# Fewer stored copies of the split delta and delta*u rows, and twice as many, shorter loads of the scan's matrices

## What is computed

```python
def step(h, inputs):
    d_t, B_t, C_t, u_t = inputs
    dA = jnp.exp(d_t[:, :, None] * A)
    h = h * dA + (d_t * u_t)[:, :, None] * B_t[:, None, :]
    y_t = jnp.einsum('bdn,bn->bd', h, C_t)
    return (h, y_t)
```

## Time and profile before

| | |
|---|---|
| median of 3 runs | 6699.06 us |
| the profiled execution's own time | 6696.66 us |
| its span in the trace | 6694.9 us |
| busy share over the span | PE 89%, DVE 82%, ACT 50%, POOL 31% |
| norm stage | about 0 to 150 us |
| project stage | about 150 to 1216 us |
| scan stage | 1216 to about 6023 us |
| output stage | the rest |

### The profile page before, as it was taken

How to read it: one execution, slowest core, us unless ns; L and a number is a source line. 1 busy time by engine, 2 the same in 40 slices (tenths; PEclk the granted TensorE clock), 3 DMA queues, 4 the chain that set the end, 5 groups by cost and what they waited for, 6 DMA issues and landing times. The chain is left out here.

```text
span 6694.9 us, 156361 instructions
## 1 busy us (share of the span) xinstructions
PE 5983.9 (89%) x46304; PEld 3510.4 (52%) x46304; DVE 5502.8 (82%) x3489; ACT 3327.8 (50%) x7459; POOL 2090.2 (31%) x6848
## 2 busy tenths in 40 slices
PE   2665664599999999999999999999999999997998
PEld 1222222355555555555555555555555555555666
DVE  7554545599999999999999999999999999983443
ACT  1544444355555555555555555555555555551111
POOL 4222223333333333333333333333333333330000
PEclk9776776799999999999999999999999999998999
DMA  4345446311111111111111111111111111113331
GB/s 143 134 161 202 168 169 205 99 38 35 38 34 38 34 38 35 38 35 38 35 37 35 38 36 37 36 37 36 36 36 36 37 36 37 35 28 130 118 104 60
DMA packets 1133185, 452.03 MB, mean 68 GB/s; under 512 B 762608, under 2 KB 1088944, under 8 KB 1132736
## 3 DMA queue, kind: packets, MB, share of 16 engines
q1 hardware_dynamic: 1121456, 438.77, 24.7%
q10 hardware_dynamic: 11664, 12.52, 0.5%
HBM read 229.72 MB, written 221.77 MB: 67 GB/s over the span
## 5 line engine op out<-in xcount | busy, mean ns | idle before, releaser
L917 DVE TENSOR_TENSOR_SCAN s_h<-s_decay,s_ubank 128x1024 f32<-128x1024 f32 x2048 | 4571.4, 2273 | 206.0 <-ACT s_ubank L891 137.9
L876 ACT ACTIVATE s_decay<-s_abank 128x512 f32<-128x512 f32 x4096 | 2219.4, 595 | 1443.9 <-PE s_abank L827 1439.3
L849 PE MATMUL s_ubank<-s_x,s_w 128*128 128x128 bf16 x16384 | 2123.7, 309 | 0.1
L812 PE MATMUL s_ybank<-s_h,s_window 128*16 128x256 f32 x16448 | 1953.6, 603 | 1.8 <-DVE s_h L917 1.8
L849 PEld LDWEIGHTS s_ubank<-s_x,s_w 128*128 128x128 bf16 x16384 | 1715.5, 129 | 74.2 <-DVE s_h L917 0.4
L827 PE MATMUL s_abank<-s_x,s_a 128*128 128x256 bf16 x8192 | 1339.1, 280 | 55.4 <-DMA s_w<-scratch_b_rows 55.4
L952 POOL TENSOR_TENSOR s_carry<-s_decay,s_h 128x32 f32<-128x32 f32 x2016 | 589.4, 292 | 2302.9 <-ACT s_decay L876 2257.7
L827 PEld LDWEIGHTS s_abank<-s_x,s_a 128*128 128x128 bf16 x8192 | 708.4, 108 | 901.3 <-issue 708.9
L812 PEld LDWEIGHTS s_ybank<-s_h,s_window 128*16 128x16 f32 x16448 | 408.2, 104 | 820.0 <-issue 817.3
L957 POOL TENSOR_TENSOR s_seed<-s_carry,s_first 128x32 f32<-128x32 f32 x2048 | 514.7, 251 | 700.1 <-ACT s_first L885 559.6
L959 POOL TENSOR_TENSOR s_decay<-s_none 128x32 f32<-128x32 f32 x2048 | 508.4, 248 | 0.3
(11 more groups left out here) (121 smaller groups left out, 3129.2 us busy)
## 6 DMA issues: line engine op xcount, KB each, us to landing
scratch_u_rows<-p_u_turn SPq DMA_DIRECT2D x136, 512.0 KB, 6.9
scratch_delta_rows<-p_dparts SPq DMA_DIRECT2D x128, 512.0 KB, 5.7
s_x<-scratch_delta_rows SPq DMA_DIRECT2D x1024, 64.0 KB, 3.5
s_x<-scratch_u_rows SPq DMA_DIRECT2D x2048, 32.0 KB, 1.7
scratch_y<-s_y SPq DMA_DIRECT2D x1036, 16.0 KB, 1.4
scratch_sz<-p_sz SPq DMA_DIRECT2D x16, 1024.0 KB, 8.7
scratch_u<-p_u SPq DMA_DIRECT2D x16, 1024.0 KB, 10.1
s_w<-scratch_b_rows SPq DMA_DIRECT2D x256, 64.0 KB, 2.4
```

The costliest lines, as they stand in the source:

```text
L812: last = nc.tensor.matmul(y_bank[32 * ct:32 * ct + WIN, 0:PAIRS], window[:, s, t * WIN:(t + 1) * WIN], H[s][:, :, t], start=(tt == 0), sto ...
L849: last = nc.tensor.matmul(dst.rearrange("p q t -> p t q"), w2[:, g, 4 * s + e, :], x2[:, s, :, e, q:q + 16], start=True, stop=True)
L876: nc.scalar.activation(decay[:, k % RING, 16 * b:16 * b + 16, :], a_bank[:, b].rearrange("p j r t -> p (j r) t"), ACT.Exp).then_inc(exp_do ...
L917: nc.vector.tensor_tensor_scan(H[s][:, PT * k:PT * k + PT, :].rearrange("p q t -> p (q t)"), decay[:, k % RING].rearrange("p q t -> p (q t)"),
```

## The change

`project_stage` stores each of delta's three parts once (3 planes), and for each token five rows of delta*u's parts, in the order 0, 1, 2, 0, 1. The products are taken in another order (i outermost), so that the parts j that they need run 0, 1, 2, 0, 1, 2, 0, 1. In the scan each load into `x1` becomes two: one of 12 partitions whose source goes twice over the three planes (an outermost dimension of stride 0 and count 2), and one of 4 partitions from the first two planes. Each load into `x2` becomes two of 8 partitions, from rows 0 to 3 and rows 1 to 4 of each token. SyncE's program in `project_stage` is rotated: what was issued before and after the loop's edge is issued in the same order as before, with the edge at another place. The semaphore counts follow.

```diff
-COMBOS = [(i, j) for j in range(3) for i in range(3) if i + j < 4]
+PARTS, PLACES = 3, 5
+COMBOS = [(i, j) for i in range(PARTS) for j in range(PARTS) if i + j < 4]
...
-                for k, (_, j) in enumerate(COMBOS):
-                    sp.dma_start(tile_of(d["delta_rows"][k], i), dparts[:, j]).then_inc(dparts_stored, 16)
+                for j in range(PARTS):
+                    sp.dma_start(tile_of(d["delta_rows"][j], i), dparts[:, j]).then_inc(dparts_stored, 16)
...
-                for k, (_, j) in enumerate(COMBOS):
-                    sp.dma_start(d["u_rows"][rows, k, :].rearrange("(s p) q -> p s q", p=P),
-                                 u_turn[:, j, :, :]).then_inc(turns_stored, 16)
+                for at in range(PLACES):
+                    sp.dma_start(d["u_rows"][rows, at, :].rearrange("(s p) q -> p s q", p=P),
+                                 u_turn[:, at % PARTS, :, :]).then_inc(turns_stored, 16)
...
             def step(i, c, b, ahead1, ahead2):
+                turn_stores(i)
+                if ahead2:
+                    front_stores(*ahead2)
                 if ahead1:
-                    front_stores(*ahead1)
-                back_stores(i, c, b)
-                turn_stores(i)
+                    back_stores(*ahead1)
             front_stores(0, 0, 0)
+            front_stores(1, 1, 0)
+            back_stores(0, 0, 0)
             over_tiles(sp, step)
...
-                for g, n, places in ((6, 2, (0, 3, 6)), (7, 1, (2, 5))):
+                for g, n, places in ((6, 2, (0, 1, 2)), (7, 1, (6, 7))):
...
-                        nc.scalar.activation(b_turn[:, :, at:at + n, :], src[:, :, :, 0:NS],
+                        nc.scalar.activation(b_turn[:, :, at:at + 3 * n - 2:3, :], src[:, :, :, 0:NS],
...
+            def thrice(src):
+
+                w = 2 * PARTS
+                twice = bass.AP(src.tensor, src.offset, [[0, 2], [src.ap[0][0], w]] + [list(a) for a in src.ap[1:]])
+                return ((0, 2 * w, twice), (2 * w, 2 * NCB, src[0:2 * NCB - 2 * w]))
...
                         src = deltas[r, :, :, :, bass.ds(f * T, 2 * T)]
-                        sp.dma_start(x1[16 * r:16 * r + 16, g, r], src).then_inc(rows_loaded[g], 16)
+                        for lo, hi, part in thrice(src):
+                            sp.dma_start(x1[16 * r + lo:16 * r + hi, g, r], part).then_inc(rows_loaded[g], 16)
...
                 for r in range(8):
-                    sp.dma_start(x2[16 * r:16 * r + 16, c % 2, r],
-                                 us[r, :, bass.ds(f * 4 + TW // 8, 4), :]).then_inc(u_loaded[c % 2], 16)
+                    for lo in range(2):
+                        sp.dma_start(x2[16 * r + 8 * lo:16 * r + 8 * lo + 8, c % 2, r],
+                                     us[r, 2 * lo:2 * lo + 8, bass.ds(f * 4 + TW // 8, 4), :]
+                                     ).then_inc(u_loaded[c % 2], 16)
...
-    scratch("delta_rows", [NCB, DI, TOK], BF16)
-    scratch("u_rows", [TOK + TW, NCB, DI], BF16)
+    scratch("delta_rows", [PARTS, DI, TOK], BF16)
+    scratch("u_rows", [TOK + TW, PLACES, DI], BF16)
```

More of the change, by code:

```diff
@@ L455, in _ @@
             sp.wait_ge(sz_stored, 16 * (NT + 1))
-            sp.wait_ge(dparts_stored, 16 * NCB * (NT + 1))
-            sp.wait_ge(turns_stored, 144 * (NT + 2))
+            sp.wait_ge(dparts_stored, 16 * PARTS * (NT + 1))
+            sp.wait_ge(turns_stored, 96 * (NT + 2))
         @block.tensor
@@ L520, in _ @@
             act.sem_inc(sz_stored, 16)
-            act.sem_inc(dparts_stored, 16 * NCB)
-            act.sem_inc(turns_stored, 144)
+            act.sem_inc(dparts_stored, 16 * PARTS)
+            act.sem_inc(turns_stored, 96)
             act.sem_inc(turn_read, 11)
@@ L571, in take_turns @@
             def take_turns(i):
-                act.wait_ge(turns_stored, i * 144 + 144)
+                act.wait_ge(turns_stored, i * 96 + 96)
                 for g in range(6):
@@ L635, in split @@
                 for src, rest, parts, free, first, whole, one, left, two in (
-                        (lw, w1, dparts, (dparts_stored, i * (16 * NCB) + 16 * NCB), delta_done, i + 2, d1_done, dr_done,
+                        (lw, w1, dparts, (dparts_stored, i * (16 * PARTS) + 16 * PARTS), delta_done, i + 2, d1_done, dr_done,
                          d2_done),
@@ L821, in logits @@
                 if k == 0 and s == 0:
-                    pe.wait_ge(rows_loaded[g], it * 176 + 176)
+                    pe.wait_ge(rows_loaded[g], it * 304 + 304)
                 for b in range(2):
@@ L835, in chunk @@
                     if k == 0:
-                        pe.wait_ge(u_loaded[s], it * 256 + (c // 2) * 128 + 128)
+                        pe.wait_ge(u_loaded[s], it * 512 + (c // 2) * 256 + 256)
                         pe.wait_ge(first_read, f + 1)
@@ L933, in lay_window @@
                 s, g = c % 2, c // 2
-                pool.wait_ge(rows_loaded[g], it * 176 + 176)
+                pool.wait_ge(rows_loaded[g], it * 304 + 304)
                 pool.wait_ge(y_ready, f + 1)
```

## The result

The kernel after takes 7505.26 us (median of 4 runs, 7504.18 to 7506.7) against 6698.69 us of the kernel before beside it: ratio 1.1205, 95% interval 1.1191 to 1.1219, +807 us. The forecast of slower, and its mechanism, came true; of the forecast +1420 us some 57% came.

The account below looks back on a forecast made before the run. The project stage was taken to wait for store bytes, the scan to be bound by TensorE, then SyncE. 6696.7 - 203 + 1600 + 22 = 8116, the median 2.4 us higher, say 8120 us; range 7150 to 9050.

Parts of the forecast that it names:

- Project stage, -203 us: Project stage: eight stores fewer per tile save 12.4 us, 198 us over 16 tiles, plus 4.6 us of final draining.
- Engines of a short load: Scan loads: the 12-row x1 load uses 2 DMA engines, the 4-row load 4, x2's halves 8.
- The x1 set, 5.93 to 22.5 us: Scan: two DMA engines' full queue holds SyncE during the x1 loads, adding 16.6 us a pair of chunks.
- The x2 issue, 0.605 us: Scan: each short x2 load takes 0.605 us to issue, 9.7 us a set for 4.0, adding 11.4 a pair.
- The pace is SyncE's sum: Scan: SyncE can't run ahead, so its 49.7 us sets the pair against TensorE's 37.12; +12.6 us, 127 times, +1600.
- The edge of the scan loop: Edge of SyncE's scan loop: no added cost was included in the forecast.
- The base: Scan before the change: two chunks take 37.12 us, of which SyncE's own work is 21.7.
- The start of the scan, +22: Scan's start: TensorE waits for the first x1 and x2 loads, 16.6 plus 5.4 us longer.
- rival B: Scan: loads spread evenly but every short DMA costs 0.80 us to issue, +9.1 us a pair, 7670 us; chance 9%.
- A: Scan: 12-row load spread over 12 engines, issues cost as now, SyncE's 33 us stays hidden, 6503 us; chance 11%.
- C: Scan: two engines carry x1 but the queue swallows the loads, SyncE isn't held; +190 us, 6706 us; chance 4%.

Follow-up runs that it names:

- h: d without the 4-row x1 loads, so the last two of the eight delta*A products are left out; 6581.69 us (one execution).
- i_interleaved: Kernel after with its x1 loads spread between the x2 loads, one row group between four x2 loads; 7515.83 us, ratio 1.122.
- c: Kernel before with only each 16-partition x2 load cut into two of 8; 6701.91 us, ratio 1.0006.
- d: Kernel after with delta*u in eight rows and x2 in 16-partition loads as before, delta's side kept; 6589.09 us, ratio 0.9838.
- e: Kernel after with the four y stores of a chunk issued by ScalarE in place of SyncE; 6734.69 us, ratio 1.0053.
- o: Kernel after with ScalarE issuing B-row loads behind an odd chunk's second and third tiles, y stores behind the fourth to seventh; 6562.7 us, ratio 0.9796.
- b: Kernel after with each 12-row x1 load written as two of six, so loads of 6, 6 and 4; 7378.04 us, ratio 1.1014.
- n: Kernel before with each 16-row x1 load's source going twice over the first four planes (outermost count 2); 6710.97 us, ratio 1.002.
- a: Kernel after with five planes of delta stored and each x1 load made of two 8-row halves, without stride 0; 6652.89 us, ratio 0.9934.
- m: e with the two B-row loads of a pair also on ScalarE, behind an odd chunk's sixth and seventh tiles; 7001.92 us, ratio 1.0454.
- f: Kernel after with five planes of delta, x1 in 8-row loads, and the y stores issued by ScalarE; 6602.96 us, ratio 0.9858.
- j: i_interleaved with the y stores also issued by ScalarE; 7007.64 us, ratio 1.0462.

## Why the prediction was right, and where its size was off

- **Project stage, -203 us**: right, -201; ScalarE's waits 70.0 us where 70 were forecast, the rate 339 GB/s.
- **Engines of a short load**: right, 2 and 4, by the count of packets.
- **The x1 set, 5.93 to 22.5 us**: 21.0 measured, for another reason than the one given. The prediction took 12.8 ns a packet from the earlier trace rows, less a queue that swallows 1.0 us (23.1 - 1.0 is 22.1, where it took 22.5). But 12.8 ns is how long one packet lasts, not how often one comes: in h it lasts 13.0 ns (17.2% of 16 engines x 11 us / 2337), which adds up to 138% of two engines' time, so packets on one engine overlap. They follow each other every 9.4 ns, so 1.82 us for a 12-row load, and 0.8 us for the 4-row load beside it, which adds its own price and not 33 packets: 8 x 2.6 = 21. Two errors, the pace of a packet and the price of the 4-row load, nearly cancelled, so that this term came out close is in part luck. That earlier loads fill the queue up, so that room for them could help, fell with i_interleaved.
- **The x2 issue, 0.605 us**: the term that failed most. It was raised by the row of line 173, a DMA with DRAM on both sides; the runs show 0.46, less than a 16-row load's 0.485. A set takes 7.4 us in the mean in place of the 9.7 forecast, twice 2.3 us a pair: 4.6 x 127 = 584 us of the forecast's excess. The nearest row would have been x2's own, which the prediction had as its lower bound.
- **The pace is SyncE's sum**: right. SyncE lost its waits for TensorE; c (hidden), d (just hidden) and e (1.7 us over) stand on either side of 37.1 us as the sum says. Moving the y stores and the B loads off SyncE (o) took the mean pair from 44.9 to 37.5 us and the ratio from 1.12 to 0.98.
- **The edge of the scan loop**: the prediction gave it nothing. The gap there is 3.1 us once in two pairs where it was 0.76 before, so +1.2 a pair, 150 us.
- **The base**: right. The mean pair before is the 37.12 us that the prediction read from one.
- **The start of the scan, +22**: +18. TensorE's first product with x2 starts 60.5 us into the scan (1075.5) where it started 42.3 us into it (1258.30).

Together: 49.7 - 1.5 (x1: 21.2 us to C's load in the mean of the 90 pairs where it was 6.1, so +15.1 in place of +16.6) - 4.6 (x2) + 1.2 (edge) = 44.8 us a pair, where 44.92 is measured. Against 37.12 that is +7.8 x 127 = 991, +18 at the start, -201: +808, against the +807 measured.

The time by itself would not have told the forecast from rival B, whose 7670 us lies nearer to 7505 than the forecast's 8120. What decides is in the trace: two and four completions, an x1 set of 21 us made of 8 dear pairs, and x2 issues of 0.46 us where B has 0.80.

The rivals: A (the loads stay hidden) fell with the 12-row load on 2 engines. Of B, half was true: an even split of x1 into 24 short loads (b) is nearly as slow as after, by the price of each issue; but x2's issues are cheap. C (SyncE isn't held) fell with the x1 set of 21 us and with SyncE's pair in every run.

## What to carry to other kernels

Before a broadcast or a shared copy is made by the load, count what the issuing queue pays: each load costs the larger of its fixed time (here 0.46 to 0.86 us, by its shape) and the pieces that fall on one DMA engine times 9.4 ns (measured here on two engines, with a source that repeats). Then add up the queue's whole program for one step and hold it against the step of the engine that sets the pace; 36.4 us under 37.1 cost nothing, 44.9 cost 12% of the whole time. A saving in one stage (201 us of stores) is worth having once the loads that pay for it are shared out over two issuing queues, each early enough for who needs it.

## What the runs showed of the hardware that was not expected

- **The time to issue goes by the fullest DMA engine.** The same 512 pieces of 128 bytes keep the queue 0.74 us when spread over 16 engines and 2.46 us over two. In this comparison the load over two engines also has a source that repeats. It is the next DMA on the queue that shows the time, so the row of a load can look harmless (0.67 us, the least at line 788) while its successor shows 1.7.
- **A long loop body on SyncE has a price at its edge.** The profile page's count of instruction traffic (packets, MB) is 39 and 0.32 before, in d and in n. In the kernel after it is:

```profile
q14 instruction: 354, 2.90, 0.1%
```

  a, b and c show 355, i 350. By the instructions of SyncE in the trace for one pass of its loop, the gap at the edge is 0.8 us in the runs with 222 (before, h, n), 254 (d), 288 (m, o) and 298 (e), and 3.0 to 3.2 us in those with 314 (f), 318 (c), 346 (i), 350 (after), 366 (a) and 382 (b). One run breaks the order: j has 296 and a gap of 2.9 us, so the number of these instructions alone doesn't settle it. In the kernel after one packet of instruction traffic starts inside each of these gaps (3019.9 to 3023.0 us: 1 packet, 0.01 MB). e, m and o still show 350 packets, with only a small gap on SyncE: there it is ScalarE's loop that has grown, from 274 to 323 instructions in e, and f and j, where both engines pay, show 666 and 661. That the gap is the fetching of the body anew is inferred from these counts; no run changed the length of a body alone.
- **Fewer rows did not make an x1 issue cheaper**: loads of 8 rows cost 0.86 us and those of 4 and 6 rows 0.83 in the mean, 16 rows 0.74, though each puts 33 packets on an engine; for x2, 8 rows cost 0.46 and 16 rows 0.485. Why the two differ in sign stays open.
